# Attention with the query projection folded into the key projection

## The reference, cut to what matters

```python
q = einsum('bsd,ed->bse', x, Wq) + bq          # 4096 x 256
k = einsum('bsd,ed->bse', x, Wk) + bk
v = einsum('bsd,ed->bse', x, Wv) + bv
scores = einsum('bqd,bkd->bqk', q, k) / sqrt(256)
out = einsum('bqk,bkd->bqd', softmax(scores, axis=2), v)
```

## Time and profile before

| | us |
|---|---|
| profiled execution | 3949.96 |
| its span | 3947.9 |
| TensorE busy | 3542.7 (90%) |
| VectorE busy | 2868.5 (73%) |
| ScalarE busy | 2432.3 (62%) |
| GpSimd busy | 1322.5 (33%) |
| projection, first load of the stage to first load of the score loop, image 0 | 1484.4 to 1567.6 |
| score loop, image 0 | 1567.6 to 2337 |
| projection, image 1 | 2337 to 2421 |
| score loop, image 1 | 2421 to 3189 |

### The profile page before, as it was taken

One profiled execution on the slowest core, in us unless ns is written; L12 is line 12 of the kernel. 1 busy time (PEld: TensorE's weight loads), 2 busy tenths in 40 slices (PEclk: granted clock), 3 DMA queues, 4 the chain that ended last, 5 costly groups with the idle time before them and its releaser, 6 DMA issues. The chain is left out here.

```text
span 3947.9 us, 81665 instructions
## 1 busy us (share of the span) xinstructions
PE 3542.7 (90%) x30559; PEld 2953.9 (75%) x30559; DVE 2868.5 (73%) x4303; ACT 2432.3 (62%) x6245; POOL 1322.5 (33%) x740
## 2 busy tenths in 40 slices
PE   8986888788869988999999979999999979788887
PEld 5644555455549986888888868888888878788886
DVE  1457999899968874677777755777777766677787
ACT  3545888788855554666656655666666632677776
POOL 0007999899955552000000001000000014222254
PEclk9988999999989998999999989999999989899999
DMA  4583111311123333000000011000000046555565
GB/s 125 172 230 78 43 41 40 80 43 43 43 61 105 118 99 112 1 17 17 17 19 25 12 53 65 17 17 17 17 17 12 12 138 213 162 137 136 139 217 169
DMA packets 204756, 303.82 MB, mean 77 GB/s; under 512 B 18464, under 2 KB 156576, under 8 KB 201376
## 3 DMA queue, kind: packets, MB, share of 16 engines
q1 hardware_dynamic: 195232, 291.51, 24.7%
q10 hardware_dynamic: 9216, 8.39, 0.6%
HBM read 199.18 MB, written 100.66 MB: 76 GB/s over the span
## 5 line engine op out<-in xcount | busy, mean ns | idle before, releaser
L661 POOL TENSOR_TENSOR mx_big<-mp_lvs,mx_big 128x1280 f32<-128x1280 f32 (+1 forms) x256 | 802.0, 3205 | 335.0 <-ACT mp_lvs L587 317.1
L640 DVE TENSOR_TENSOR mx_big<-mp_psL,mx_big 128x2816 f32<-128x2816 f32 (+1 forms) x256 | 786.6, 3147 | 39.1 <-PE mp_psO L532 32.1
L594 ACT ACTIVATE mp_cut<-mp_psO,mx_mask 128x128 f32<-128x128 f32 x2048 | 551.0, 404 | 145.1 <-PE mp_psO L532 114.6
L532 PE MATMUL mp_psO<-mx_big,mp_pair 128*16 128x256 f32 x8192 | 501.5, 385 | 107.6 <-DVE mx_big L640 75.0
L1298 PE MATMUL sv_psO<-at_v_hi,sv_p_hi 128*128 128x258 f32 x2048 | 583.2, 285 | 13.2 <-DVE sv_p_lo L1386 10.1
L1298 PE MATMUL sv_psO<-at_v_lo,sv_p_hi 128*128 128x258 f32 x2048 | 578.1, 282 | 0.0
L1298 PE MATMUL sv_psO<-at_v_hi,sv_p_lo 128*128 128x258 f32 x2048 | 577.9, 282 | 0.0
L1317 ACT COPY sv_S<-sv_psS 128x512 f32<-128x512 f32 x512 | 300.5, 587 | 378.4 <-PE sv_psS L1272 260.7
L532 PEld LDWEIGHTS mp_psO<-mx_big,mp_pair 128*16 128x16 f32 x8192 | 330.1, 126 | 242.5 <-DVE mx_big L640 135.9
L1361 DVE TENSOR_TENSOR sv_run<-sv_run,sv_S 128x512 f32<-128x512 f32 x448 | 314.5, 702 | 248.1 <-ACT sv_S L1317 247.0
L1386 DVE TENSOR_TENSOR sv_p_lo<-sv_S,sv_p_hi 128x512 fp32r<-128x512 f32 x512 | 353.8, 691 | 108.4 <-ACT sv_p_hi L1326 107.4
(11 more groups left out here) (244 smaller groups left out, 7446.7 us busy)
## 6 DMA issues: line engine op xcount, KB each, us to landing
re_xg<-xg SPq DMA_DIRECT2D x192, 384.0 KB, 3.3
xg<-ga_xg SPq DMA_DIRECT2D x32, 768.0 KB, 4.0
att<-mx_big SPq DMA_DIRECT2D x16, 1024.0 KB, 5.5
mx_big<-rv SPq DMA_DIRECT2D x16, 1024.0 KB, 17.4
mp_pair<-att SPq DMA_DIRECT2D x128, 128.0 KB, 2.9
fr_xr<-in_x SPq DMA_DIRECT2D x16, 512.0 KB, 4.7
fr_xl<-in_x SPq DMA_DIRECT2D x32, 256.0 KB, 4.3
rv<-fr_rvs SPq DMA_DIRECT2D x16, 512.0 KB, 3.0
```

The source lines that it names most:

```text
L532: mm = pe.matmul(psO[32 * j:32 * j + 2 * H, c % 2, q, :], pair[:, s, :, :, c * YC + y], Z[:, c % 2, y, :], start=True, stop=True, tile_pos ...
L594: ins = nc.scalar.activation(cut[:, s, c, :, h * DK:(h + 1) * DK], psO[:, c % 2, :, h * DK:(h + 1) * DK], ACT.Copy, scale=mask[:, h:h + 1])
L640: nc.vector.tensor_tensor(Z[:, c % 2, 0:m], psL[:, s, 0:D].unsqueeze(1).broadcast_to([P, m, D]), big[:, rv_slot(b, c), 0:m], ALU.mult).the ...
L661: nc.gpsimd.tensor_tensor(Z[:, c % 2, m:YC], lvs[:, s, :].unsqueeze(1).broadcast_to([P, YC - m, D]), big[:, rv_slot(b, c), m:YC], ALU.mult ...
```

## The change

The scores of query token x and key token y are `(Wq x + bq) . (Wk y + bk)`. The change computes them as `x . (M y + g) + (kbw . y + kb0)`, where `M = Wq' Wk` (the prime is the transpose), `g = Wq' bk`, `kbw = Wk' bq` and `kb0 = bq . bk`.

- Tokens themselves stand on the query side. There is no query projection, no `qs`, no tensor q in DRAM. In the projection block the splits of x blocks 0 and 1 are written straight to `q_hi`, `q_lo` (`xh`, `xo`), and the score loop loads blocks 2 to 7 from `xlT_d`.
- One projection with `M` makes the keys, with bias `g`. Its PSUM tile `psP` is now doubled by block, and TensorE waits for the evictions of two blocks before.
- The value weight gets two columns more, the first with `kbw`, the second zero, so the value matmuls also make `kbw . y`. VectorE adds `kb0` and puts it into `kb`, one number for each key (`kb_made`). ScalarE's eviction of the scores becomes an Identity with that number as the bias of the partition.
- Image 0 makes `M`, `g`, `kbw`, `kb0` on TensorE from the weights given (`fold`) and stores them in DRAM; image 1 loads them. Loads have semaphores of their own, and the identity, the bias row and the value weight are waited for later than the key weight.

```diff
+            small = pj.sb("small", [P, 2 * KT + 1])
+            gb, kbw, kb0 = small[:, 0:KT], small[:, KT:2 * KT], small[:, 2 * KT:2 * KT + 1]
...
+            psP = pj.ps("psP", [P, 2, KT, BLK])
+            psV = pj.ps("psV", [P, KB, 512])
...
+            def xh(n):
+
+                return q_hi[:, n] if n < 2 else x_hi[:, n % 2]
+
+            def xo(n):
+                return q_lo[:, n] if n < 2 else x_lo[:, n % 2]
...
+                    if b == 0:
+                        with nc.allow_non_contiguous_dma("two biases of 256 numbers, one to a partition"):
+                            sp.dma_start(ident[:, :], ident_d).then_inc(ident_in, 16)
+                            sp.dma_start(wq[:, :, :], k_rows(wqT)).then_inc(fold_in, 16)
+                            sp.dma_start(wk[:, :, :], k_rows(wkT)).then_inc(fold_in, 16)
+                            sp.dma_start(bqc[:, :], bq.rearrange("(k p) -> p k", p=P)).then_inc(fold_in, 16)
+                            sp.dma_start(bkc[:, :], bk.rearrange("(k p) -> p k", p=P)).then_inc(fold_in, 16)
                         load(0)
-                        for dst, src in loads:
-                            sp.dma_start(dst, src).then_inc(w_in, 16)
+                    else:
+                        load(0)
+                        sp.dma_start(mt[:, :, :], mt_d).then_inc(fold_in, 16)
+                        sp.dma_start(small[:, :], small_d).then_inc(fold_in, 16)
+                    sp.dma_start(wv[:, :, 0:D], k_rows(wvT)).then_inc(v_in, 16)
...
+                    sp.dma_start(bvr[:, :], bv.rearrange("(o n) -> o n", o=1).broadcast_to([P, D])).then_inc(b_in, 16)
+                    if b > 0:
+                        sp.dma_start(ident[:, :], ident_d).then_inc(ident_in, 16)
...
+                    if b == 0:
+                        sp.wait_ge(mt_made, 1)
+                        sp.wait_ge(small_made, 1)
+                        sp.dma_start(mt_d, mt[:, :, :]).then_inc(mt_out, 16)
+                        sp.dma_start(small_d, small[:, :]).then_inc(mt_out, 16)
+                        sp.wait_ge(mt_out, 32)
...
+                    def fold():
+
+                        pe.wait_ge(ident_in, 16)
+                        pe.wait_ge(fold_in, 64)
+                        for e, w in enumerate((wk, wq)):
+                            for o in range(KT):
+                                for k in range(KT):
+                                    mm = pe.transpose(psP[:, 1, e, o * D + k * P:o * D + (k + 1) * P], w[:, k, o * P:(o + 1) * P], ident[:, :])
+                            mm.then_inc(w_turned, 1)
+                        pe.wait_ge(wo_kept, 2)
+                        for m in range(KT):
+                            for o in range(KT):
+                                pe.matmul(psV[:, 0, m * D:(m + 1) * D], wko[:, o, m * P:(m + 1) * P], wqo[:, o, :], start=(o == 0), stop=(o == KT - 1))
+                        for m in range(KT):
+                            for o in range(KT):
+                                pe.matmul(psV[:, 1, m:m + 1], wqo[:, o, m * P:(m + 1) * P], bkc[:, o:o + 1], start=(o == 0), stop=(o == KT - 1))
+                        for m in range(KT):
+                            for o in range(KT):
+                                pe.matmul(psV[:, 1, KT + m:KT + m + 1], wko[:, o, m * P:(m + 1) * P], bqc[:, o:o + 1], start=(o == 0), stop=(o == KT - 1))
+                        for o in range(KT):
+                            mm = pe.matmul(psV[:, 1, 2 * KT:2 * KT + 1], bqc[:, o:o + 1].broadcast_to([P, P]), bkc[:, o:o + 1], start=(o == 0), stop=(o == KT - 1))
+                        mm.then_inc(folded, 1)
...
+                    for n in range(NBLK):
+                        pe.wait_ge(x_cut, n + 1)
+                        pe.wait_ge(mt_cut, 1)
+                        reach(pe, k_lo_kept, (n - 1) * KT)
+                        reach(pe, k_hi_kept, (n - 1) * KT)
+                        terms = [(a, x, k) for k in range(KT) for a, x in ((mt_hi, xh(n)), (mt_hi, xo(n)), (mt_lo, xh(n)))]
...
-                        for m, mm in units(1, KT, s):
+                                mm = pe.matmul(psP[:, n % 2, m, :], a[:, k, m * P:(m + 1) * P], x[:, k, :], start=(i == 0), stop=(i == len(terms) - 1))
                             mm.then_inc(k_made, 1)
...
+                        pe.wait_ge(wv_cut, 1)
+                        terms = [(x, a, k) for k in range(KT) for x, a in ((xh(n), wv_hi), (xh(n), wv_lo), (xo(n), wv_hi))]
                         for u in range(2):
                             reach(pe, v_biased, (n - 1) * 2 + u + 1)
+                            reach(pe, kb_made, (n - 1) * 2 + u + 1)
                             for t in (2 * u, 2 * u + 1):
                                 for i, (x, a, k) in enumerate(terms):
-                                    mm = pe.matmul(psV[:, t, :], x[:, s, k, t * P:(t + 1) * P], a[:, k, :], start=(i == 0), stop=(i == len(terms) - 1))
+                                    mm = pe.matmul(psV[:, t, 0:VW], x[:, k, t * P:(t + 1) * P], a[:, k, :], start=(i == 0), stop=(i == len(terms) - 1))
                             mm.then_inc(v_made, 1)
...
+
+                    if b == 0:
+                        for e, w in enumerate((wko, wqo)):
+                            act.wait_ge(w_turned, e + 1)
+                            nc.scalar.copy(w[:, :, :], psP[:, 1, e, :].rearrange("p (o i) -> p o i", o=KT)).then_inc(wo_kept, 1)
...
+                    if b == 0:
+                        act.wait_ge(folded, 1)
+                        nc.scalar.copy(mt[:, :, :], psV[:, 0, :].rearrange("p (k i) -> p k i", k=KT)).then_inc(mt_made, 1)
+                        act.wait_ge(mt_made, 1)
+                    else:
+                        act.wait_ge(fold_in, 32)
+                    nc.scalar.copy(mt_hi[:, :, :], mt[:, :, :]).then_inc(mt_hi_cut, 1)
+                    act.wait_ge(v_in, 16)
+                    act.wait_ge(wv_ended, 2)
+                    nc.scalar.copy(wv_hi[:, :, :], wv[:, :, :]).then_inc(wv_hi_cut, 1)
...
-                            nc.scalar.activation(k_hi[:, j, n * BLK:(n + 1) * BLK], psP[:, KT + j, :], ACT.Identity,
-                                                 bias=bias[1][:, j:j + 1]).then_inc(k_hi_kept, 1)
+                            nc.scalar.activation(k_hi[:, j, n * BLK:(n + 1) * BLK], psP[:, n % 2, j, :], ACT.Identity,
+                                                 bias=gb[:, j:j + 1]).then_inc(k_hi_kept, 1)
...
-                        if n == 1:
-                            pool.wait_ge(q_kept, KT)
-                            nc.gpsimd.tensor_copy(q_hi[:, 0], qs[:, 0]).then_inc(q0_hi_cut, 1)
-                            pool.wait_ge(q0_hi_cut, 1)
-                            nc.gpsimd.tensor_tensor(q_lo[:, 0], qs[:, 0], q_hi[:, 0], ALU.subtract).then_inc(q0_cut, 1)
...
-                        nc.vector.tensor_tensor(x_lo[:, n % 2], xs[:, n % 2], x_hi[:, n % 2], ALU.subtract).then_inc(x_cut, 1)
-
+                        nc.vector.tensor_tensor(xo(n), xs[:, n % 2], xh(n), ALU.subtract).then_inc(x_cut, 1)
...
-                    for j in range(3):
-                        dve.wait_ge(w_hi_cut, j + 1)
-                        nc.vector.tensor_tensor(w_lo[j][:, :, :], w[j][:, :, :], w_hi[j][:, :, :], ALU.subtract).then_inc(w_cut, 1)
+                    if b == 0:
+                        dve.wait_ge(folded, 1)
+                        nc.vector.tensor_copy(small[:, :], psV[:, 1, 0:2 * KT + 1]).then_inc(small_made, 1)
+                        dve.wait_ge(small_made, 1)
+                    else:
+                        dve.wait_ge(fold_in, 32)
+                    dve.wait_ge(wv_ended, 1)
+                    nc.vector.tensor_copy(wv[:, :, D], kbw).then_inc(wv_ended, 1)
+                    dve.wait_ge(mt_hi_cut, 1)
+                    nc.vector.tensor_tensor(mt_lo[:, :, :], mt[:, :, :], mt_hi[:, :, :], ALU.subtract).then_inc(mt_cut, 1)
+                    dve.wait_ge(wv_hi_cut, 1)
+                    nc.vector.tensor_tensor(wv_lo[:, :, :], wv[:, :, :], wv_hi[:, :, :], ALU.subtract).then_inc(wv_cut, 1)
...
+                            nc.vector.tensor_scalar(kb[:, n * KB + 2 * u:n * KB + 2 * u + 2], psV[:, 2 * u:2 * u + 2, D], kb0, None, ALU.add).then_inc(kb_made, 1)
```

In the score loop:

```diff
-                        reach(sp, q_cut, n - 1)
-                        sp.dma_start(q[:, :, :], q_d[:, :, n * BLK:(n + 1) * BLK].rearrange("k p t -> p k t")).then_inc(q_in, 16)
...
+                        reach(sp, q_cut, n - 2)
+                        sp.dma_start(q[:, :, :], xlT_d[:, :, TAIL][:, :, n * BLK:(n + 1) * BLK].rearrange("k p t -> p k t")).then_inc(q_in, 16)
+
+                    load_q(2)
...
-                        if n + 2 < NBLK:
+                        if 0 < n < NBLK - 2:
...
-                    for n in range(1, NBLK):
-                        pool.wait_ge(q_in, n * 16)
+                    for n in range(2, NBLK):
+                        pool.wait_ge(q_in, (n - 1) * 16)
...
```

(40 more changed lines are left out.)

63 lines of the change are left out of this document (27 added, 36 removed).

## The result

The changed kernel took 3915.3 us (median of 4 runs, 3907.6 to 3919.9) against 3951.1 us (4 runs, 3945.7 to 3955.0) for the one before: a ratio of 0.9908, 95% interval 0.9887 to 0.9930. The forecast was 3914, the range 3903 to 3930. The profiled execution took 3916.6 us, with a span of 3914.8, 33.1 less than the span before.

What follows compares the result with a forecast made beforehand. TensorE was taken to bound the projection stages. -44.0 + 1.0 + 4.0 + 4.1 - 2.9 + 2.9 = -34.9 us from the profiled 3949.96 gave 3915.1, less 1.5 for the median: 3914 us, range 3903 to 3930.

Steps and rivals of the forecast that it cites:

- Query projection, -44.0: Projection stages: 12 query matmuls x 8 blocks x 2 images at 0.229 us leave TensorE, 44.0 us less.
- Value width, +1.0: Projection stages: value matmuls two columns wider cost 0.5 us per image, +1.0 us.
- VectorE and GpSimd, +4.0: Projection blocks: VectorE, waiting for GpSimd, has rounds of 6.2 us against TensorE's 5.49; 2.0 us lost per image.
- rival 1: Projection stages: VectorE and GpSimd become the bound, late rounds 7.8 us, 10 us lost per stage, 3930 us; chance 0.13.
- Fold, +4.1: Start of image 0's projection: folding the weights puts the first matmul 14.9 us after the first load, against 10.8.
- Second image, -2.9: Start of image 1's projection: with the product loaded, TensorE starts 7.5 us after the first load, against 10.38.
- Key bias, +2.9: Score loop: eviction 0.091 us longer, seen only where TensorE waits at a turn, 32 x 0.09 us.
- Rival 2: Score loop has no room for the 0.091 us, all 512 units pay: 3957 us; chance 0.03 in full, 0.03 in part.
- Hand-overs between stages, 0: Between stages: seven more semaphores cleared per image, put at 0, at most 1 us per image.
- rival 3: Recurrent stage: changed rounding makes its test fail and 32 more steps run, 187 us more, 4101 us; chance 0.02.
- rival 4: Everything small goes well: rounds of 5.5 us, fold +2, second image -4, bias free, 3903 us; chance 0.07.

Runs made afterwards that it cites:

- the 256-column kernel: Changed kernel with value matmuls of 256 columns instead of 258, a stand-in loaded for the weight product, and no key bias: 3905.8 us in one timed execution.
- the second pair: Second profiles of the kernel before and the changed kernel, unedited: first matmul 10.33 to 15.74 us (image 0), 10.24 to 7.23 (image 1).
- two copies more: Changed kernel with two small 128x1 ScalarE copies added behind every eviction of the score loop: 3918.6 us, loops 766.2 and 765.8 us.
- short queries: Kernel before with ten of the twelve query matmuls of each block left out: 3912.6 us, ratio 0.9909.

## Why the prediction was right, step by step

**Query projection, -44.0: right.** Removing five sixths of it alone saved 17.6 us per image, where 18.3 was to come. No other engine set the stage; VectorE's lag took 0.2 to 0.35 of the difference.

**Value width, +1.0: the size was wrong, and so was its cause.** The matmuls of both kinds stand wider apart, 0.2343 and 0.1196 against 0.2287 to 0.2300 and 0.1143 to 0.1178. 96 x 0.005 + 192 x 0.0035 is 1.2 us per image, instead of 0.5. The two columns aren't it, as the 256-column kernel shows, and no run here says what is.

**VectorE and GpSimd, +4.0: the mechanism was right, the term mis-sized; it measured 0.5.** VectorE's round is 6.08 us (`x_lo` to `x_lo`: 1522.65, 1528.73), where 6.2 was predicted, and `x_lo` ends 1.08 after GpSimd, as in the earlier trace rows. But TensorE's own round is 5.68, not 5.49. The lag per late round is then 0.40 and not 0.71. From the end of the first `x_lo` of the loop (1512.28) to that of the last (1542.68) five rounds take 30.4 us and TensorE's five 28.4, so VectorE falls 2.0 behind, not 3.05. The slack, which I had put at 1.05, was 1.8 (the first of these blocks started at 1514.06) and held most of it: 0.26 us is seen, in front of the last block only. The stage without GpSimd's subtraction shows both parts, 0.56 us in `x_lo` and 0.26 in front of the last block. The price of rival 1 was high by its own terms: four rounds of 7.8 and one of 5.7 against 5.49, less the slack, are 8.4 us and not 10.

**Fold, +4.1: measured +5.1, a size.** The weights came sooner (4.95 after the first load for 6.2) and the last three steps took their 2.1. The transposes and the copy took 2.62, as forecast. But the product took 3.57 us instead of 1.8: its four matmuls are eight entries in the trace, two to each f32 matmul, at 0.45. The 16 entries of the earlier trace rows were eight matmuls, and I had counted them as 16. The same slip is in the one-column matmuls: ten are 20 entries, which at the 0.22 of the earlier trace rows would be 4.4 us. They took 2.68 where 2.2 was forecast, and only because the granted clock, 0.50 from the transposes to the end of the product, was 1.00 from 1496 to 1499. In the kernel with the plain copy as eviction it stayed at 0.50; there the same ten took 4.27 us, and the first key matmul came 17.11 us after the first load. Without the fold the start is at 6.85, so the fold costs 9.1 by itself; the old start of 10.8 hid the rest.

**Second image, -2.9: measured -3.2,** and -3.0 in the second pair. Right.

**Key bias, +2.9: right in sum, half right in place.** The loops grew by 1.4 per image (mean 763.9 in six loops with the queries of before, 765.3 in four of the changed kernel; 0.9 to 2.3 from pair to pair), of which about 1.0 goes with the eviction; it is 0.102 us longer. By the Trainium skill (ScalarE: Activation LUTs, What ACT_TABLE_LOAD costs) a pointer operand adds about 93 ns, and this agrees. The wait before a turn grew by 0.3 us an image in 7 waits, not in 16, and the plain copy gave back only 0.1 of it; `p_lo` holds TensorE 0.4 longer, and the rest is spread. Rival 2 would have needed the room to be gone, and with two copies more it wasn't.

**Hand-overs between stages, 0: wrong.** TensorE's sequencer wait at the score loop's start is 5.2 us, before 4.4; GpSimd's end to the next load is 2.16, before 1.73. The tail of each stage grew by 0.9 us. Of that 0.43 lies behind GpSimd's end, where the prediction had put seven more semaphores at 0 and at most 1; 0.34 is GpSimd ending later behind the last `v`, since its two `v_lo` now stand back to back (2.31 us for the pair), and the rest is before that `v`. No run took the semaphores away, so the first part is not shown to be theirs.

**Not in it at all: the clock.** TensorE starts each projection stage at a granted clock of 0.50 (of 1.2 and 2.4 GHz, the lower). After the fold it had been idle for 2.14 us and was at 0.50 again for all of 1500 to 1505. The first block of image 0 took 8.56, 8.53, 8.40, 8.28 and 7.05 us in five executions of one and the same projection stage, and 8.52 with no fold ahead, so the fold isn't shown to be what makes it long. Here +0.95 and -0.9 cancelled; in the second pair they did not (+1.4 and -0.1).

So the main term and the signs of the others were right, but that the sum hit so closely was luck: its errors cancelled. It came out 1.8 too low against the spans: the lag took 3.5 less; the blocks 1.2, the fold 1.0, the tails 1.8, the score stages 1.2 and everything else 0.1 more. Rival 1 did not appear, though its rule is at work in `x_lo`; rival 3 did not (192 loads of the recurrence, as before); rival 4 had the lag nearly right and the rest wrong.

## What to carry to other kernels

A product of weights that is made once is dear by its place: ahead of the first matmul it cost 9 us, in idle stretches of the stage before it cost 1. When matmuls go, take the remaining spacing from several executions and price each rival engine against that round, since the lag is a difference of two near numbers. An engine with idle time took more work for nothing here; an operation that a chain waits for can cost something even there, of the order of 1 us in 765 in this case. And the first block behind a pause varies by 1.5 us between executions, so a claim of that size needs several profiles.

## What the runs showed of the hardware

- Matmuls of one shape, at a granted clock of 1.00 and with TensorE never idle, follow each other at three different spacings: 0.2287 and 0.1143 us, 0.2300 and 0.1178 (both in the kernel before, exchanged between images in two executions), and 0.233 to 0.235 and 0.119 to 0.120 in all stages of the changed kernel and its variants. Width, bank layout, GpSimd's work and how densely the others work don't set it. A spacing can also change within a stage: with short queries one block of image 0 had its value matmuls at 0.1177 between blocks at 0.114. The score loop stands at 0.230 to 0.231 and 0.120 in both. The cause is open.
- The same block of work right after a start at the lower clock took 8.56 or 7.05 us in kernels with the same projection stage, at a mean granted clock of 0.64 or 0.80, by when the clock rose.
- A VectorE subtraction with both inputs in SBUF that overlaps a GpSimd subtraction ends later by nearly all of the overlap: 128x1024 took 1.79 us for 1.23, with 0.71 of overlap; 128x512 took 0.98 for 0.69, with 0.43.
- An f32 matmul of 256 columns leaves two entries in the trace, 0.45 us apart at the lower clock and 0.226 at the higher; an f32 transpose of 128x128 leaves one.
